# Phase differences in the first convolution, and the group 2 and 3 attention work placed between the first gates

## The chip, the cores and the metric

One core of one Trainium2 chip runs the whole kernel. The metric is the device time of one execution in microseconds; a lower time is better. The median of three runs is the time of a kernel, and one execution was recorded by the hardware profiler.

## The reference, cut to what matters

64 graphs of 128 nodes with 128 features each, all float32. Layer 0 is a gated update that reads a convolution and an attention over each graph; layer 1 is an adjacency product.

```python
h = maximum(layernorm(x), 0)
# layer 0, per graph
c  = relu(bn1(conv1(h)))            # kernel size 1
c  = relu(bn2(conv2(c)) + h)        # kernel size 17, padding 8: x_conv
s  = h @ w_se.T + b_se              # three coordinates per node
A  = exp(-dist(s, s)) * adj
nmp = A @ relu(h @ w_msg.T + b_msg)
gi, gh = [c, nmp] @ w_ih.T + b_ih, h @ w_hh.T + b_hh
r, z = sigmoid(gi_r + gh_r), sigmoid(gi_z + gh_z)
n = tanh(gi_n + r * gh_n)
x = x + (1 - z) * n + z * h
# layer 1
h = maximum(layernorm(x), 0)
x = x + adj @ (h @ weight) + bias
```

## The kernel before

**Tiles and groups.** Four graphs make a group (512 columns), so there are 16 groups. Two groups, 2t and 2t+1, are convolved together (8 graphs). The body is an opening, which brings in groups 0 to 3 and convolves groups 0 and 1, then seven steps `step(t)`, t = 1 to 7, and an ending. Step t convolves and gates groups 2t and 2t+1, brings in groups 2t+2 and 2t+3 (turn, first convolution, messages, rows, distances, neighbour sums) and finishes groups 2t-2 and 2t-1. Each product that needs accuracy is made of three TensorE passes: the operands are split in a rounded part (`_hi`, made by ScalarE) and the rest (`_lo`, made by VectorE).

**The convolution.** The nodes of a graph are stored by phase, that is by node number modulo 4, in `c1` (4 phases with 8 graphs). The 17 taps are stored by their number modulo 4: A0, A1, A2, A3 hold four taps each and T16 the last. In the steps the convolution is computed from sums of taps (M22, M12, M32, M21, M23) and differences of phases (`px`, made by GpSimd in `pre`), with fewer products. In the opening it is computed tap by tap: `direct(tap)` adds one tap to the banks pQ (even output phases) and pP (odd ones), each 512 columns wide: three passes a bank at 512 columns, or six at 256. There are 17 taps and two banks, so 34 bank products of three passes. The rounded weights live in `conv_hi`, the rests in `conv_lo`; `W_PARTS` says in which pieces they are split (`round_w` on ScalarE, `split_w` on VectorE). GpSimd makes the sums of taps in `sum_phases`.

**Order.** Every engine works off one written list in order: `opening()`, `step(t)` and `ending()` exist once for TensorE (`pe`), ScalarE (`act`), VectorE (`dve`) and GpSimd (`pool`). An instruction waits for semaphores (`wait_ge`, `have`), and everything behind it on its engine waits with it. SyncE issues the loads; those of x groups 5 to 7 wait for `gate_split`.

**Names for the steps below.** For a group g: `first(g)` (ScalarE) normalises into `hn`; `x_turn(g)` (TensorE) turns it; `hidden(g)` is `hidden_graphs` and `hidden_rows` (three ScalarE instructions); `hidden_lo(g)` (VectorE); `conv1(g)` and `conv1_out(g)`; `messages(g)` (TensorE, then ScalarE) with `place_bias(g)` and `coordinates(g)`; `pair_rows(g)` (nine small VectorE instructions), `rows_turn(g)`, `left_rows(g)`, `right_rows(g)`, `distances(g)`, `decay(g)`, `masked(g)`, `neighbour_sums(g)`, `sums_hi(g)`, `sums_lo(g)`; the gates `gates_h`, `gates_n`, `gates_c` (nine passes each), `hidden_gate`, `reset_gate`, `update_gate`, `candidate`, `blend_start(g)` and `blend_end(g)` (VectorE, three and two instructions), `o_turn(g)`, `residual(g)`. `normalise1([a, b])` (VectorE) takes the statistics of two groups, `scale1` (GpSimd) their power -0.5 and `shift1` (VectorE) the offset that `first` needs.

```python
def x_turn(g):
    have(pe, hn_set, g + 1)
    if g % 2 == 0:
        have(pe, nlo_set, g if g > 2 else 0)
        have(pe, hlo_set, 1 if g == 2 else 0)
```

## Time and profile before

| | |
|---|---|
| median of 3 runs | 346.11 us (343.37 to 346.34) |
| the profiled execution | 344.95 us, of which the span from the first to the last instruction is 342.6 us |
| TensorE passes | busy 329.8 us, 96% of the span, 2198 instructions |
| VectorE | busy 261.6 us, 76%, 735 instructions |
| ScalarE | busy 220.5 us, 64%, 431 instructions |
| GpSimd | busy 152.1 us, 44%, 131 instructions |
| mean granted TensorE clock | 0.995 of full speed |

A share is the busy time of an engine over the span. Since an engine works off its list in order, a share does not say which engine holds the others; the idle times with their releasers and the chain of waits do.

### The profile page before, as it was taken

How to read it: one execution, taken by the hardware profiler on the slowest of the kernel's cores; microseconds unless marked ns; L12 is line 12 of the kernel's file. 1: busy time of each engine (PE TensorE's matmuls, PEld its weight loads, DVE VectorE, ACT ScalarE, POOL GpSimd, SP SyncE). 2: the span in 40 equal slices, each digit the busy share in tenths (PEclk: the TensorE clock that was granted, in tenths of full speed). 3: DMA queues.
4: the chain of work that ended last, by engine and by line, in shares of the span. 5: the costliest groups of instructions: out<-in, count | busy, mean ns of one | idle time of the engine just before them, and what ended most of it. 6: DMA issues, size and time to landing. Idle time of an engine off the chain costs nothing.

```text
span 342.6 us, 6310 instructions
## 1 busy us (share of the span) xinstructions
PE 329.8 (96%) x2198; PEld 296.3 (86%) x2198; DVE 261.6 (76%) x735; ACT 220.5 (64%) x431; POOL 152.1 (44%) x131
## 2 busy tenths in 40 slices
PE   7699979999999999999999999999999999999995
PEld 5489958799988999899988999889988998899894
DVE  5576896899688995899688995899687895784474
ACT  2938835876865876676865876676866763444353
POOL 7053271024952189024952189024950189029014
PEclk9989999999999999999999999999999999999999
DMA  7900020001220022001210023001100000000003
GB/s 234 340 5 0 6 89 0 2 1 33 92 64 0 2 83 76 29 0 33 94 62 0 2 71 114 2 0 33 64 32 2 0 33 31 2 1 2 0 1 123
DMA packets 7951, 15.02 MB, mean 44 GB/s; under 512 B 1008, under 2 KB 1648, under 8 KB 7792
## 3 DMA queue, kind: packets, MB, share of 16 engines
q1 hardware_dynamic: 7776, 14.62, 12.7%
q8 instruction: 17, 0.28, 0.4%
q14 instruction: 14, 0.11, 0.1%
q10 hardware_dynamic: 144, 0.01, 0.0%
HBM read 10.43 MB, written 4.19 MB: 43 GB/s over the span
## 4 chain that ended last, share of the span: by engine, by line
PE 65%; DVE 19%; ACT 9%; issue 4%; POOL 1%; DMA 1%; POOLq 0%; DVEq 0%; ACTq 0%
PE pQ L311 4%; PE pQ L312 4%; PE pQ L313 4%; PE pNR L311 4%; PE pNR L313 4%; PE pNR L312 4%; PE pF L424 4%; PE pP L311 4%; PE pP L312 4%; PE pP L313 4%; DVE st L981 3%; ACT work L750 2%; PE pZ L484 2%; PE pI L313 2%; PE pI L311 2%
## 5 line engine op out<-in xcount | busy, mean ns | idle before, releaser
L1331 POOL TENSOR_TENSOR rs<-ve,neg_half 128x4 f32<-128x4 f32 x15 | 15.6, 1040 | 90.6 <-DVE ve L1111 90.6
L1326 POOL TENSOR_TENSOR rs<-ve,neg_half 128x8 f32<-128x8 f32 (+1 forms) x9 | 15.5, 1721 | 73.1 <-DVE ve L988 73.1
L311 PE MATMUL pP<-cx_hi,conv_hi 128*128 128x256 f32 x154 | 45.0, 292 | 0.0
L313 PE MATMUL pP<-cx_hi,conv_lo 128*128 128x256 f32 x154 | 43.5, 282 | 0.0
L312 PE MATMUL pP<-cx_lo,conv_hi 128*128 128x256 f32 x154 | 43.3, 281 | 0.0
L311 PE MATMUL pQ<-cx_hi,conv_hi 128*128 128x256 f32 x126 | 37.0, 293 | 0.0
L750 ACT ACTIVATE work<-work,nb,rs 128x128 f32<-128x128 f32 x60 | 24.8, 483 | 17.5 <-DVE nb L1115 17.0
L312 PE MATMUL pQ<-cx_lo,conv_hi 128*128 128x256 f32 x126 | 35.4, 281 | 0.0
L313 PE MATMUL pQ<-cx_hi,conv_lo 128*128 128x256 f32 x126 | 35.3, 281 | 0.0
L311 PEld LDWEIGHTS pP<-cx_hi,conv_hi 128*128 128x128 f32 x154 | 29.1, 189 | 0.3
L312 PEld LDWEIGHTS pP<-cx_lo,conv_hi 128*128 128x128 f32 x154 | 29.1, 189 | 0.3
L313 PEld LDWEIGHTS pP<-cx_hi,conv_lo 128*128 128x128 f32 x154 | 29.0, 188 | 0.0
L1069 DVE TENSOR_TENSOR cx_lo<-px,cx_hi 128x576 fp32r<-128x576 f32 x28 | 27.2, 1008 | 0.8 <-ACT cx_hi L664 0.8
L312 PEld LDWEIGHTS pQ<-cx_lo,conv_hi 128*128 128x128 f32 x126 | 23.8, 189 | 0.3
L311 PEld LDWEIGHTS pQ<-cx_hi,conv_hi 128*128 128x128 f32 x126 | 23.8, 189 | 0.0
L313 PEld LDWEIGHTS pQ<-cx_hi,conv_lo 128*128 128x128 f32 x126 | 23.7, 188 | 0.0
L770 ACT ACTIVATE work<-pNR,rz_b 128x512 f32<-128x512 f32 x16 | 11.0, 689 | 19.5 <-PE pNR L313 19.0
L683 ACT ACTIVATE hn<-x_ring,nb,rs 128x128 f32<-128x128 f32 x56 | 22.5, 485 | 0.0
L1379 POOL TENSOR_TENSOR x_ring<-work,late 128x512 f32<-128x512 f32 x16 | 20.5, 1284 | 0.3 <-DVE nb L1279 0.3
L664 ACT ACTIVATE cx_hi<-px 128x576 fp32r<-128x576 f32 x28 | 17.6, 674 | 3.5 <-POOL px L966 3.1
L399 PEld LDWEIGHTS pNR<-early,hn 128*128 128x128 f32 x128 | 16.3, 189 | 3.0 <-issue 2.1
L779 ACT ACTIVATE work<-work,vec 128x512 f32<-128x512 f32 x16 | 11.6, 724 | 11.2 <-DVE work L1083 11.2
(287 smaller groups left out, 1058.0 us busy)
## 6 DMA issues: line engine op xcount, KB each, us to landing
x_ring<-x_in SPq DMA_DIRECT2D x16, 256.0 KB, 2.8
adj_ring<-adj_in SPq DMA_DIRECT2D x16, 256.0 KB, 3.0
out<-x_ring SPq DMA_DIRECT2D x15, 256.0 KB, 2.0
work<-conv_in SPq DMA_DIRECT2D x1, 1088.0 KB, 7.6
x_ring<-gate_in SPq DMA_DIRECT2D x1, 576.0 KB, 7.7
out<-x_ring SPq DMA_DIRECT2D x2, 128.0 KB, 1.8
early<-early_in SPq DMA_DIRECT2D x1, 129.5 KB, 4.5
late<-late_in SPq DMA_DIRECT2D x1, 128.0 KB, 7.9
```

The lines of the kernel that those rows point to most:

```text
L311: pe.matmul(acc, w_hi, m_hi, start=start, stop=False)
L312: pe.matmul(acc, w_hi, m_lo, start=False, stop=False)
L313: return pe.matmul(acc, w_lo, m_hi, start=False, stop=stop)
L399: last = pe.matmul(ms[:, j, 0:MS], graph(hn[g % 2], j), w_ms, start=False, stop=True, skip_group_check=True)
L424: last = pe.matmul(lane(sums_bank(g)[:], j), graph(msg[g % 2], j), graph(att[g % 2], j), start=True, stop=True)
L664: act.activation(cx_hi[:, CX_PARTS[k][0]:CX_PARTS[k][1]], cx_source(k), ACT.Copy).then_inc(cxhi_set, 1)
L683: last = act.activation(graph(hn[g % 2], j), xs(g, j), ACT.Identity, bias=nb1[:, i:i + 1], scale=rs1[:, i:i + 1])
L750: last = act.activation(graph(h2[g % 2], j), graph(x1[g % 2], j), ACT.Relu, bias=nb2[g % 2][:, j:j + 1], scale=rs2[g % 2][:, j:j + 1])
L1069: dve.tensor_tensor(cx_lo[:, part], cx_source(k), cx_hi[:, part].bitcast(F32), ALU.subtract)\
L1326: pool.tensor_tensor(rs1[:, lane], ve1[:, lane], neg_half[:, lane], ALU.pow).then_inc(rs1_set, 1)
L1331: pool.tensor_tensor(rs2[g % 2][:], ve2[g % 2][:], neg_half[:, 0:GG], ALU.pow).then_inc(rs2_set, 1)
L1379: pool.tensor_tensor(xs(g).rearrange("p (g d) -> p g d", g=GG), x1[g % 2].rearrange("p (g d) -> p g d", g=GG), l1_bias, ALU.add).then_inc( ...
```

## The change

The first convolution (groups 0 and 1) goes over to phase differences: one sum of taps is formed from A0+A1 and A2+A3 (stored at M21, M23), `even_tap` applies the even taps to the difference of phases (8 bank products into pQ), `sum_tap` applies the summed taps to the odd phases (8, into pP), T16 is added, VectorE adds what pP holds to both `base` tiles (`with_sum`), and then `odd_tap` writes pP anew (8, with T16). So there are 26 bank products of three passes. VectorE makes the two differences (`less_odd`, `next_less_odd`) and all sums of taps (`sum_odd`, `sum_halves`), which GpSimd no longer does. Four pieces of `cx` are split instead of two, and the weights in seven parts instead of six. The row turns, distances and neighbour sums of groups 2 and 3 move from the middle of the tap products to places between the gates of groups 0 and 1 on TensorE, and the lists of ScalarE, VectorE and GpSimd are put in a new order with them. In the diff below the indentation is cut by eight; in the lists of the openings the removed lines are left out ("..."), as they stand in the listing above.

```diff
@@ -234,22 +235,36 @@
 def taps(n, first=0):
     return slice(first * D, (first + n) * D)
-W_PARTS = (taps(8, A0), taps(8, A2), taps(1, T16), taps(4, M22), taps(8, M12), taps(8, M21))
-W_SUMS = (0, 0, 0, 2, 2, 3)
+W_PARTS = (taps(4, A0), taps(4, A2), taps(1, T16), taps(8, M21), None, taps(4, M22), taps(8, M12))
+W_SUMS = (0, 0, 0, 1, 0, 3, 2)
+def w_part(w, k):
+    if k == 4:
+        return w[:, taps(16, A0)].rearrange("p (a b w) -> p b a w", a=2, b=2)[:, 1]
+    return w[:, W_PARTS[k]]
 CX_PARTS = ((X22, X22 + 1), (X12, X21 + 1), (X32, X23 + 1), (X11, X31 + 1), (X13, X33 + 1))
 CX_PRES = (0, 1, 2, 4, 5)
-FIRST_ORDER = (0, 3, 4, 1, 2)
-SLOT = (0, 2, 1, 3)
+FIRST_FILLS = (None, 3, 4, 0, 4)
 CX_FILLS = (0, 1, 2, 4, 4)
 def cx_before(t):
-    return 2 + 5 * (t - 1) if t else 0
+    return 4 + 5 * (t - 1) if t else 0
 def pre_before(t):
     return 5 * (t - 1) if t else 0
+FIRST_AT = (X11, X32, X12, X13)
+def first_source(k):
+    return (px[:, 0:2], c1[:, 2:4], c1[:, 0:2], px[:, 2:4])[k]
+def first_place(t, k):
+    return t[:, FIRST_AT[k]:FIRST_AT[k] + 2]
 def cx_source(k):
...
@@ -320,24 +335,27 @@
                                  start=j == 0, stop=j == len(weights) - 1)
         return last
-    def direct(tap, start=False, stop=False):
-        w = T16 if tap == 16 else 4 * (tap % 4) + tap // 4
+    def half_rate(bank, part, w, j, start=False, stop=False):
         w_hi, w_lo = conv_hi[:, w * D:(w + 1) * D], conv_lo[:, w * D:(w + 1) * D]
-        ends = []
-        for e, bank in enumerate((pQ, pP)):
-            at_even, at_odd = e + tap, e + 2 + tap
-            slots = [SLOT[at_even % 4], SLOT[at_odd % 4]]
-            if slots[1] == slots[0] + 1 and at_even // 4 == at_odd // 4:
-                parts = [(bank[:], slice(slots[0], slots[0] + 2), at_even // 4)]
-            else:
-                parts = [(bank[:, 0:CG * QN], slice(slots[0], slots[0] + 1), at_even // 4),
-                         (bank[:, CG * QN:], slice(slots[1], slots[1] + 1), at_odd // 4)]
-            for acc, phases, at in parts:
-                m_hi, m_lo = cx_hi[:, phases, :, at * GG:at * GG + QW], cx_lo[:, phases, :, at * GG:at * GG + QW]
-                ends.append((pe.matmul(acc, w_hi, m_hi, start=start, stop=False),
-                             pe.matmul(acc, w_hi, m_lo, start=False, stop=False),
-                             pe.matmul(acc, w_lo, m_hi, start=False, stop=stop)))
-        return ends
+        x = FIRST_AT[part]
+        if j % 2 == 0:
+            parts = [(bank[:], slice(x, x + 2), j // 2)]
+        else:
+            parts = [(bank[:, 0:CG * QN], slice(x + 1, x + 2), j // 2),
+                     (bank[:, CG * QN:], slice(x, x + 1), j // 2 + 1)]
+        for acc, phases, at in parts:
+            last = split_product(acc, w_hi, w_lo, cx_hi[:, phases, :, at * GG:at * GG + QW],
+                                 cx_lo[:, phases, :, at * GG:at * GG + QW], start, stop)
+        return last
+    def even_tap(j):
+        return half_rate(pQ, 0, (A0, A2)[j % 2] + j // 2, j, start=j == 0)
+    def sum_tap(j):
+        return half_rate(pP, 1, (M21, M23)[j % 2] + j // 2, j, start=j == 0, stop=j == 6)
+    def odd_tap(j):
+        return half_rate(pP, 3, (A1, A3)[j % 2] + j // 2, j, start=j == 0)
     def four(first, more=False):
...
@@ -377,6 +395,7 @@
             have(pe, hlo_set, 1 if g == 2 else 0)
         elif g > 1:
             have(pe, hlo_set, g)
+            have(pe, hG_set, g)
         for j in range(GG):
             last = pe.transpose(lane(turn_bank(g)[:], j), graph(hn[g % 2], j), ident[:])
         last.then_inc(hT_placed, 1)
@@ -404,6 +423,7 @@
         have(pe, pair_set, g + 1)
         if g % 2 == 0 and g > 1:
             have(pe, hlo_set, g + 2)
+            have(pe, hG_set, g + 2)
         elif g > 1:
             have(pe, c1_set, g + 1)
...
@@ -507,63 +527,73 @@
         messages(0)
         keep_clock(6)
         pe.wait_ge(w_split, 1)
+        pe.wait_ge(cxlo_set, 1)
+        even_tap(0)
+        even_tap(2)
+        even_tap(4)
+        even_tap(6)
+        messages(1)
+        pe.wait_ge(w_split, 2)
+        even_tap(1)
+        even_tap(3)
+        even_tap(5)
+        even_tap(7).then_inc(f_done[0], 1)
+        pe.wait_ge(w_split, 4)
         pe.wait_ge(cxlo_set, 2)
...
+        sum_tap(0)
         rows_turn(0)
...
+        sum_tap(2)
+        sum_tap(4)
+        rows_turn(1)
+        sum_tap(1)
+        distances(0)
+        sum_tap(3)
+        distances(1)
+        sum_tap(5)
+        sum_tap(7)
+        neighbour_sums(0)
+        sum_tap(6).then_inc(f_done[1], 1)
+        pe.wait_ge(cxlo_set, 3)
+        half_rate(pQ, 2, T16, 8, stop=True).then_inc(f_done[3], 1)
+        neighbour_sums(1)
         x_turn(2)
...
+        pe.wait_ge(w_split, 5)
+        pe.wait_ge(cxlo_set, 4)
+        pe.wait_ge(t0_set, 2)
+        odd_tap(0)
+        odd_tap(2)
+        odd_tap(4)
         conv1(2)
...
+        x_turn(3)
+        odd_tap(6)
         messages(2)
...
+        odd_tap(1)
+        odd_tap(3)
         conv1(3)
...
+        odd_tap(5)
         messages(3)
+        odd_tap(7)
+        half_rate(pP, 1, T16, 8, stop=True).then_inc(f_done[4], 1)
+        gates_h(0)
         rows_turn(2)
...
+        gates_n(0)
         distances(2)
...
+        gates_c(0)
         rows_turn(3)
...
+        gates_h(1)
+        neighbour_sums(2)
         distances(3)
...
+        gates_n(1)
         neighbour_sums(3)
...
+        gates_c(1)
+        o_turn(0)
         x_turn(4)
...
+            pe.wait_ge(w_split, 7)
...
-        elif k in (1, 2):
-            have(act, f_done[4], 1)
+        elif k:
+            act.wait_ge(f_done[FIRST_FILLS[k]], 1)
         act.activation(cx_hi[:, CX_PARTS[k][0]:CX_PARTS[k][1]], cx_source(k), ACT.Copy).then_inc(cxhi_set, 1)
-    def split_hi_phases(e):
-        act.wait_ge(c1_set, 2)
-        act.activation(cx_hi[:, 2 * e:2 * e + 2], c1[:, 2 * e:2 * e + 2], ACT.Copy).then_inc(cxhi_set, 1)
+    def split_hi_first(k):
+        if k in (0, 3):
+            act.wait_ge(diff_set, 2 if k else 1)
+        else:
+            act.wait_ge(c1_set, 2)
+        act.activation(first_place(cx_hi, k), first_source(k), ACT.Copy).then_inc(cxhi_set, 1)
...
-        have(act, hlo_set, g + 1 if g < 2 else 0)
+        have(act, hlo_set, g + 1 if g < 4 else 0)
         act.activation(hn[g % 2][:].rearrange("p (g n) -> p g n", g=GG),
                        turn_bank(g)[:].rearrange("p (n g) -> p g n", g=GG), ACT.Relu).then_inc(hG_set, 1)
...
-            have(act, cxlo_set, cx_before(g // 2 - 1) + 1 if g > 2 else g)
+            have(act, cxlo_set, (0, 3, cx_before(g // 2 - 1) + 1)[min(g // 2, 2)])
+            have(act, diff_set, g if g == 2 else 0)
...
         place_bias(0)
         hidden_graphs(0)
         conv1_out(0)
...
+        conv1_out(1)
         act.wait_ge(conv_loaded, 16)
         round_w(0)
...
+        split_hi_first(0)
+        hidden_graphs(1)
         round_w(1)
...
         messages(0)
         place_bias(1)
+        split_hi_first(1)
+        round_w(2)
+        round_w(3)
+        split_hi_first(2)
         residual_phases(0)
...
         residual_phases(1)
         act.wait_ge(gate_loaded, 16)
         act.activation(gate_hi[:], gate, ACT.Copy).then_inc(gate_rounded, 1)
         first(2)
+        messages(1)
+        place_bias(2)
         left_rows(0)
...
         left_rows(1)
         decay(0)
...
+        first(3)
+        round_w(4)
+        decay(1)
+        split_hi_first(3)
+        sums_hi(0)
+        hidden_rows(2)
+        sums_hi(1)
+        hidden_graphs(2)
         conv1_out(2)
...
         messages(2)
         place_bias(3)
+        hidden_rows(3)
+        hidden_graphs(3)
+        conv1_out(3)
+        conv_round(0, 0)
+        messages(3)
+        split_hi(1, 0)
         round_w(5)
...
+        conv_round(0, 1)
+        hidden_gate(0)
         left_rows(2)
         decay(2)
...
         reset_gate(0)
         update_gate(0)
         candidate(0)
+        left_rows(3)
+        round_w(6)
+        hidden_gate(1)
+        sums_hi(2)
+        decay(3)
         split_hi(1, 1)
         split_hi(1, 2)
...
+        first(4)
+        sums_hi(3)
+        split_hi(1, 3)
         reset_gate(1)
         place_bias(4)
         update_gate(1)
+        hidden(4)
+        first(5)
+        split_hi(1, 4)
...
-    have(eng, cxlo_set, cx_before(t) if t > 1 else 0)
+    have(eng, cxlo_set, cx_before(t))
...
-    def split_lo_phases(e):
-        have(dve, cxhi_set, e + 1)
-        dve.tensor_tensor(cx_lo[:, 2 * e:2 * e + 2], c1[:, 2 * e:2 * e + 2], cx_hi[:, 2 * e:2 * e + 2].bitcast(F32),
-                          ALU.subtract).then_inc(cxlo_set, 1)
+    def split_lo_first(k):
+        dve.wait_ge(cxhi_set, k + 1)
+        dve.tensor_tensor(first_place(cx_lo, k), first_source(k), first_place(cx_hi, k).bitcast(F32), ALU.subtract)\
+           .then_inc(cxlo_set, 1)
+    def less_odd():
+        dve.wait_ge(c1_set, 2)
+        dve.tensor_tensor(px[:, 0:2], c1[:, 0:2], c1[:, 2:4], ALU.subtract).then_inc(diff_set, 1)
+    def next_less_odd():
+        dve.tensor_tensor(px[:, 2:3], c1[:, 1:2], c1[:, 2:3], ALU.subtract)
+        dve.tensor_tensor(px[:, 3:4, :, 0:QR - GG], c1[:, 0:1, :, GG:QR], c1[:, 3:4, :, 0:QR - GG], ALU.subtract)\
+           .then_inc(diff_set, 1)
+    def sum_odd():
+        dve.wait_ge(conv_loaded, 16)
+        two_by_two = conv[:, taps(16, A0)].rearrange("p (a b w) -> p a b w", a=2, b=2)
+        dve.tensor_tensor(conv[:, taps(8, M21)].rearrange("p (a w) -> p a w", a=2), two_by_two[:, :, 0],
+                          two_by_two[:, :, 1], ALU.add).then_inc(wsum_set, 1)
+    def sum_halves():
+        dve.tensor_tensor(conv[:, taps(8, M12)], conv[:, taps(8, A0)], conv[:, taps(8, A2)], ALU.add)\
+           .then_inc(wsum_set, 1)
+        dve.wait_ge(wsum_set, 2)
+        dve.tensor_tensor(conv[:, taps(4, M22)], conv[:, taps(4, M12)], conv[:, taps(4, M32)], ALU.add)\
+           .then_inc(wsum_set, 1)
+    def with_sum(e):
+        dve.wait_ge(f_done[1], 1)
+        dve.wait_ge((sumE_set, sumO_set)[e], 1)
+        dve.scalar_tensor_tensor(base[e][:], phases(1), bn_a[:, 1:2], base[e][:], ALU.mult, ALU.add).then_inc(t0_set, 1)
     def split_lo(t, k):
-        have(dve, cxhi_set, cx_before(t) + (FIRST_ORDER.index(k) if t == 1 else k) + 1)
+        have(dve, cxhi_set, cx_before(t) + k + 1)
         part = slice(*CX_PARTS[k])
         dve.tensor_tensor(cx_lo[:, part], cx_source(k), cx_hi[:, part].bitcast(F32), ALU.subtract)\
            .then_inc(cxlo_set, 1)
     def split_w(k):
         have(dve, w_rounded, k + 1)
-        dve.tensor_tensor(conv_lo[:, W_PARTS[k]], conv[:, W_PARTS[k]], conv_hi[:, W_PARTS[k]].bitcast(F32),
-                          ALU.subtract).then_inc(w_split, 1)
+        dve.tensor_tensor(w_part(conv_lo, k), w_part(conv, k), w_part(conv_hi, k).bitcast(F32), ALU.subtract).then_inc(w_split, 1)
     def blend_start(g):
...
         dve.tensor_tensor(zh[g % 2], zh[g % 2], cand[g % 2], ALU.subtract).then_inc(oT_set, 1)
     def residual(g):
+        if g == 0:
+            dve.wait_ge(w_split, 7)
         have(dve, o_placed, g + 1)
         have(dve, h2_set, g - 1)
         have(dve, x1b_set, g - 1)
@@ -1123,6 +1190,7 @@
     def conv_out(t, e):
         have(dve, f_done[3 + e], t + 1)
         have(dve, (sumE_set, sumO_set)[e], t + 1)
+        have(dve, t0_set, 0 if t else e + 1)
         dve.scalar_tensor_tensor(phases(e), phases(e), bn_a[:, 1:2], base[e][:], ALU.mult, ALU.add).then_inc(ct_set, 1)
...
         apply1(1)
         hidden_lo(0)
         hidden_lo(1)
+        sum_odd()
+        less_odd()
         split_w(0)
...
+        split_lo_first(0)
         coordinates(0)
         split_w(1)
         normalise1([2, 3])
         split_w(2)
+        split_w(3)
+        coordinates(1)
+        split_lo_first(1)
+        shift1([2, 3])
         pair_rows(0)
...
+        dve.wait_ge(gate_rounded, 1)
+        dve.tensor_tensor(gate_lo[:], gate, gate_hi[:].bitcast(F32), ALU.subtract).then_inc(gate_split, 1)
         pair_rows(1)
         right_rows(0)
+        next_less_odd()
+        right_rows(1)
+        split_lo_first(2)
+        masked(0)
+        split_w(4)
+        masked(1)
+        split_lo_first(3)
+        sums_lo(0)
+        with_sum(0)
+        with_sum(1)
         hidden_lo(2)
...
+        sums_lo(1)
         coordinates(2)
...
+        pair_rows(2)
         hidden_lo(3)
...
+        conv_out(0, 0)
+        sum_halves()
         coordinates(3)
+        conv_lo_out(0, 0)
+        conv_out(0, 1)
+        split_lo(1, 0)
+        conv_lo_out(0, 1)
         right_rows(2)
         pair_rows(3)
...
         masked(2)
+        split_w(5)
+        blend_start(0)
         right_rows(3)
+        blend_end(0)
+        sums_lo(2)
         normalise1([4, 5])
         masked(3)
...
         shift1([4, 5])
...
+        split_w(6)
         sums_lo(3)
...
         split_lo(1, 1)
         split_lo(1, 2)
...
+        residual(0)
         hidden_lo(4)
...
+        split_lo(1, 3)
+        split_lo(1, 4)
         normalise1([6, 7])
...
@@ -1361,17 +1438,6 @@
     pool.wait_ge(bnb_set, 1)
     pool.tensor_scalar(bn_half[:], bn_b[:, 1:2], 0.5, None, ALU.mult).then_inc(vecs_set, 1)
-    def sum_phases():
-        pool.wait_ge(conv_loaded, 16)
-        pool.tensor_tensor(conv[:, taps(8, M12)], conv[:, taps(8, A0)], conv[:, taps(8, A2)], ALU.add)\
-            .then_inc(wsum_set, 1)
-        pool.wait_ge(wsum_set, 1)
-        pool.tensor_tensor(conv[:, taps(4, M22)], conv[:, taps(4, M12)], conv[:, taps(4, M32)], ALU.add)\
-            .then_inc(wsum_set, 1)
-        two = conv[:, taps(16, A0)].rearrange("p (a b w) -> p a b w", a=2, b=2)
-        pool.tensor_tensor(conv[:, taps(8, M21)].rearrange("p (a w) -> p a w", a=2), two[:, :, 0], two[:, :, 1],
-                           ALU.add).then_inc(wsum_set, 1)
     def with_bias(g):
         have(pool, x1_set, g + 1)
         if g == 0:
@@ -1397,15 +1463,13 @@
             .then_inc(sumO_set, 1)
     def opening():
-        pool.wait_ge(cxlo_set, 2)
         scale1([2, 3])
-        sum_phases()
-        pre(pool, 1, 1)
-        pre(pool, 1, 2)
         pool.wait_ge(pair_set, 4)
-        for k in range(3, 6):
+        for k in range(1, 4):
             pre(pool, 1, k)
         scale1([4, 5])
+        for k in range(4, 6):
+            pre(pool, 1, k)
```

## Rows read from the trace of the kernel before

**Rows 1.** Windows: busy us of each engine, granted clock, DMA share, GB/s
```profile
...
18.30:20.00 1.70, 1.70 (x5) 1.32 (x4) 1.67 (x13) 0.46 (x1) 0.00 (x0) 0.51 0.00 0
20.00:21.70 1.70, 1.70 (x5) 1.32 (x4) 1.53 (x14) 0.00 (x0) 1.08 (x1) 0.50 0.04 10
...
69.44:108.00 38.56, 38.41 (x266) 35.01 (x265) 31.52 (x91) 27.16 (x55) 19.11 (x14) 1.00 0.13 42
...
```

**Rows 2.** Timeline of TensorE: start us, us, line, operation, tiles, [idle before <-releaser]
```profile
...
16.87 0.47 PE L337 MATMUL pQ<-cx_hi,conv_hi 128*128 128x512 f32 x1 [2.13 <-DVE cx_lo L1063]
...
22.68 1.05 PE L399 MATMUL pNR<-early,hn 128*128 128x131 f32 x8
...
24.96 0.40 PE L337 MATMUL pQ<-cx_hi,conv_hi 128*128 128x512 f32 x1
...
26.36 0.40 PE L337 MATMUL pQ<-cx_hi,conv_hi 128*128 128x512 f32 x1
...
44.96 0.47 PE L415 MATMUL pF<-right,left 128*128 128x512 f32 x1 [0.53 <-ACT left L737]
...
50.35 0.50 PE L415 MATMUL pH<-right,left 128*128 128x512 f32 x1 [2.00 <-ACT left L737]
...
54.39 0.40 PE L311 MATMUL pNR<-h_hi,gate_hi 128*128 128x512 f32 x1
...
69.44 0.28 PE L311 MATMUL pP<-cx_hi,conv_hi 128*128 128x256 f32 x1
...
71.21 0.60 PE L381 MATMUL pF<-ident,hn 128*128 128x128 f32 x4
...
75.04 0.66 PE L474 MATMUL pI<-ident,work 128*128 128x128 f32 x4
...
```

**Rows 3.** Timeline of VectorE, same columns
```profile
...
13.92 1.22 DVE L1074 TENSOR_TENSOR conv_lo<-work,conv_hi 128x1024 fp32r<-128x1024 f32 x1 [2.42 <-ACT conv_hi L676]
15.30 1.43 DVE L1063 TENSOR_TENSOR cx_lo<-c,cx_hi 128x576 fp32r<-128x576 f32 x2 [0.16 <-ACT cx_hi L668]
...
17.96 1.64 DVE L981 BATCH_NORM_STATS2 st<-x_ring 128x6 f32<-128x128 f32 x8
...
24.98 1.07 DVE L1028 CAST svx<-sv 128x16 fp32r<-128x16 f32 x1
26.08 2.33 DVE L1030 TENSOR_TENSOR svx<-sv,svx 128x16 fp32r<-128x16 f32 x1
...
38.49 0.16 DVE L1024 TENSOR_TENSOR sq<-sv 128x12 f32<-128x12 f32 x1
...
39.72 0.68 DVE L1059 TENSOR_TENSOR n_lo<-pZ,n_hi 128x512 fp32r<-128x512 f32 x1
...
70.57 0.69 DVE L1080 SCALAR_TENSOR_TENSOR work<-work 128x512 f32<-128x512 f32 x1
...
73.50 0.69 DVE L1092 TENSOR_TENSOR work<-work 128x512 f32<-128x512 f32 x1
...
```

**Rows 4.** Timeline of ScalarE
```profile
...
12.80 1.08 ACT L676 ACTIVATE conv_hi<-work 128x1024 fp32r<-128x1024 f32 x1
...
14.59 1.26 ACT L668 ACTIVATE cx_hi<-c 128x576 fp32r<-128x576 f32 x2
...
65.44 0.59 ACT L699 ACTIVATE h_hi<-pF 128x512 fp32r<-128x512 f32 x1
...
66.39 1.65 ACT L683 ACTIVATE hn<-x_ring,nb,rs 128x128 f32<-128x128 f32 x4
...
```

**Rows 5.** Timeline of GpSimd
```profile
...
24.72 1.30 POOL L1369 TENSOR_TENSOR work<-work 128x512 f32<-128x512 f32 x1
25.97 2.41 POOL L1372 TENSOR_TENSOR work<-work 128x1024 f32<-128x1024 f32 x1
...
46.52 1.42 POOL L964 TENSOR_TENSOR ac<-c 128x576 f32<-128x576 f32 x1 [1.27 <-DVE pair L1039]
...
51.13 1.65 POOL L1326 TENSOR_TENSOR rs<-ve,neg_half 128x8 f32<-128x8 f32 x1 [0.37 <-DVE ve L988]
...
```

101 lines of the change are left out of this document (3 added, 98 removed).

## Prediction

> **What bounds the kernel now.** I read the page first: TensorE is busy for 96% of the span, the others for 44 to 76%. Then windows: in the first step it is busy for 38.41 of 38.56 us [rows 1], so the steps hold nothing that a lost microsecond could be made up from. What TensorE gains or loses before or inside step 1 stays in the total. The change touches only the stretch up to there. The timeline of TensorE gives its milestones [rows 2]: the tap products start at 16.87, the gates of group 0 at 54.39, step 1 at 69.44, x_turn(5) at 71.21, o_turn(1) at 75.04. Its losses are the idle 2.13 ahead of the first product, waits of 0.53 and 2.00 for the left rows of groups 2 and 3, and the stretch at half clock from about 18.3 to 21.7 (0.51 and 0.50 granted [rows 1]), where seven to eight passes took 0.43 instead of 0.23, a loss of 1.6. VectorE's timeline shows that group 1's blend starts at 70.57 and ends at 74.19 (73.50 + 0.69 [rows 3]), 0.85 ahead of o_turn(1): that margin is the first thing a late VectorE eats.
>
> **Prices.** All are distances from start to start. Six passes of 512 columns take 1.40 (24.96 to 26.36 [rows 2]), so a bank product of three is 0.70; six passes of 256 columns are taken the same. The eight message passes take 0.81 [rows 2] and a little behind them, 0.9; neighbour sums, which are eight passes too, the same. For VectorE: 1024 columns 1.14 to 1.22, 576 columns 0.67 to 0.75, 512 columns 0.60 to 0.69, the statistics of two groups 2.43 (17.96 to 20.39, of which 1.64 is in the row), a pair_rows 1.25 (38.49 to 39.72) [rows 3]. For ScalarE: 1024 columns 0.95 to 1.08, 576 columns 0.58, 512 columns 0.49 to 0.60, one first(g) 1.55 to 1.65 [rows 4]. GpSimd: 1.42 for a difference of phases, 1.65 for the power of eight [rows 5]. I lay the new lists of the four engines side by side, starting each instruction at the later of its engine and what it waits for.
>
> **TensorE up to the first gates.** The start moves: c1 of group 1 is ready at 13.3 since its hidden_graphs is put behind it, less_odd 0.75, rounding 0.7, the rest 0.75, and the first product starts at 15.75, 1.1 earlier. Before, 54.39 - 16.87 = 37.5 were 34 x 0.70 = 23.8 of products, 1.6 of clock, 2.5 of waits and 9.6 of other work, of which 1.7 (rows, distances, neighbour sums of groups 2 and 3) is moved behind. After: 15.75 + 26 x 0.70 (18.2) + 7.9, plus new waits. With idle time of only 1.1 ahead I count no clock loss. The waits: 0.55 for pair_rows(1) and 0.35 for right_rows(1), behind the gate_lo split and next_less_odd on VectorE; 0.5 for masked(1), which stands behind split_w(4), and that behind ScalarE's first(3) and round_w(4), done at 29.7; 1.25 before odd_tap(0), because both with_sum (0.66 each) must have read pP and stand behind masked(1), split_lo_first(3) and sums_lo(0): done at 34.15; 2.2 before conv1(3). That last one is a new wait in a queue: ScalarE does messages(2), then place_bias(3), then hidden_rows(3). TensorE ends messages(2) at 39.3, coordinates 0.1, the two ScalarE steps 1.3, hidden_rows twice 0.49, hidden_lo(3) 0.7: 42.6, and TensorE was ready at 40.5. Sum 4.85, so the gates of group 0 start at 46.5 to 46.7, 7.8 earlier than 54.39.
>
> **Between the gates.** The distances of group 2 are done only at 51.25, behind gates_n(0); before, everything of groups 2 and 3 was over by 57. Now VectorE and ScalarE carry rows, decays, masks, blend, splits and the statistics of groups 4 and 5 at the same time. Group 0's last gate is done at 53.3, the candidate at 55.3. Behind it ScalarE has left_rows(3) 0.16, round_w(6) 0.95, hidden_gate(1) 0.57, sums_hi(2) 0.59: 57.5. VectorE then does sums_lo(2) 0.6, normalise1([4, 5]) 2.43, masked(3) 0.7: 61.2. TensorE was ready for neighbour_sums(3) at 58.6: a wait of 2.7. Next, GpSimd's power of groups 4 and 5 (1.65) ends at 62.4, shift1 at 62.6, first(4) at 64.3, sums_hi(3) at 64.8, sums_lo(3) at 65.55; x_turn(4), moved behind o_turn(0), waits 0.8 for it. Step 1 starts at 66.1, now 3.3 ahead of 69.44. The weights' last split (M12, 63.8) is in time.
>
> **Step 1.** ScalarE goes on without a gap from 62.7: split 0.6, reset_gate(1) 0.63, place_bias(4) 0.65, update_gate(1) 0.63, hidden(4) 1.5, first(5) 1.65: 70.2. The change put hidden(4) and first(5) behind all of these. TensorE reaches x_turn(5) at 67.85 and waits to 70.3, 2.5 long; that is already 0.9 ahead only. VectorE meanwhile waits for hidden(4) to 68.7 and, in split_lo(1, 4), for first(5) and the split behind it to 70.8: 71.5. Then normalise1([6, 7]) 2.43, blend_start(1) and blend_end(1) 3.6: 77.6, against 74.19 before. TensorE has done conv1(4), messages(4) and the M12 product by 74.2 and waits 3.5 for o_turn(1): 77.7, 2.6 behind 75.04. hidden_lo(5) and place_bias(5) come late too, 1.0 against 0.2: 3.4 to 3.5 behind. From there the lists are those of before and every engine is late by like amounts.
>
> **What the layout leaves out.** Laid out in the same way, the kernel before (with its 1.6 of clock) comes to the gates, to step 1 and to o_turn(1) 1.1 too early each, so the like-for-like difference is +4.5. Left out as well is that VectorE and GpSimd block one another: svx's 16 elements took 2.33 and ended at 28.41, when GpSimd's addition ended (28.38), and the one before it 1.07, up to the end of the addition at 26.02 [rows 3, 5]. Moving sum_phases to VectorE takes these away (3 us of VectorE, where it had time to spare) for 1.22 + 1.22 + 0.6 of VectorE's own, where it has less. In the new order GpSimd's three differences run from 51.0 to 55.3 beside split_w(5) and blend_start(0), and two more run beside shift1 and split_w(6). Each meeting costs up to 1.42 [rows 5], four of them 5.4; what a meeting costs before as well goes off, and with all of them in both layouts the difference is +6.3. The bounds of this are 0 and 1.8, and I take a third of it, since the order in which two lists meet shifts by tenths: +5.0. The span goes from 342.6 to 347.6; with the 2.35 around it that is 350.0. The sum stands on the profiled 344.95, which is 1.2 under the median of 346.11 and inside the spread of the three runs.
>
> **The other small edits.** One more weight piece and two more cx pieces cost ScalarE 1.2 and VectorE 1.4, and sit in the queues above. Loads of x groups 5 to 7 are issued behind gate_lo, at 24 instead of 41.7; nobody waits for them, and they hide behind the products. The hG waits on turns of later groups are met earlier by hlo: nothing.
>
> **A rule of the Trainium skill.** After 2.13 idle the clock fell; after 2.00 idle at 50.35 [rows 2] it did not. The Trainium skill (TensorE: Matmul & The Clock Gate, "Part 1: The HAM clock gate") says that the engine falls to half clock once it has been idle, and gets it back by being busy. By that rule the four new waits of over 2 us are each exposed to another 1.6, and one or two of them would bring the sum to 351.6 or 353.2.
>
> **Rivals.** (1) Forecast, VectorE and ScalarE late in the first gates and in step 1, 348 to 352: 0.55. (2) More than that: a clock drop behind one of the waits (1.6, the loss of the row at half clock) or all meetings with GpSimd (1.8 on the 4.5), 352 to 356: 0.13. For it speak the long waits; against it, that a pass at half clock ahead of a wait only shortens the wait. (3) About the same: normalise1([6, 7]) and split_lo(1, 4) do not hold the blend, because first(4) and first(5) come 2 us earlier than I have them; then o_turn(1) waits 1 to 1.5 and the sum is +2 to +2.5, 347: 0.15. The layout's error of 1.1 over 50 us leaves room for that. (4) Faster: TensorE keeps its lead at step 1. Its work is 5.6 smaller (8 x 0.70), it starts 1.1 earlier, and the clock loss may go. If first(5) is there by 67.9 and group 1's blend by 74.2 - 2.5 = 71.7, the lead of 3.3, less the 1.1, stays: 342.8; if the new waits between the gates go as well, up to 5.6 + 1.1 + 1.6 = 8.3 are won: 336.7. It decides in VectorE's list: the blend would have to end six microseconds before my 77.6. For it speaks that VectorE has 12 us of waits in the opening of before; against it, that 7 us of new work take much of that and that the waits of the new order are for ScalarE and TensorE, which extra room doesn't shorten: 0.17. That the products would not shrink is excluded by the count of 26.
>
> **Numbers.** The predicted time is that of (1), 350.0. The range runs from 344.5 to 355: it leaves out (4) and the end of (2). A median of this kernel tells about 1% (3.5 us) from no change. Faster by over 1%, under 342.6: most of (4), 0.13. Slower by over 1%, over 349.6, would be half of (1) if the time were spread evenly around 350, but its mechanism leans up by the clock and GpSimd, so with (2) I give 0.55. The rest is 0.32.
>
> **What the profile after would show.** First product near 15.8 and no half-clock stretch; the first of the nine gate passes of group 0 near 46.6; a wait of 2 us before conv1(3) put down to h_lo; a wait of 2.7 before neighbour_sums(3) put down to att; step 1 near 66 to 67; waits at x_turn(5) (hn) and at o_turn(1) (work); group 1's blend ending at 77 to 79; then steps of 38.6. Wrong would make me: the blend of group 1 before 73, or an order on ScalarE in which first(4) is not held by the statistics of groups 4 and 5.

## The result, and the profile after

After: 353.51 us, the median of 5 runs (352.50 to 354.76). Before, beside it: 344.80 us (5 runs, 343.37 to 346.34). The ratio is 1.0231 with an interval of 1.0192 to 1.027, so the change made the kernel slower by about 8.7 us, where 5.0 was forecast. The profiled execution of after took 353.09 us, its span 351.3.

The page of after: span, busy time, granted clock in 40 slices.
```profile
span 351.3 us, 6261 instructions
...
PE 329.3 (94%) x2162; PEld 294.9 (84%) x2162; DVE 267.5 (76%) x746; ACT 222.2 (63%) x434; POOL 146.2 (42%) x128
...
PEclk9899999896999999999999999999999999999999
```
TensorE is now idle for 22 us of the span, and the clock row has dips in the slices of 8.8 us that begin at 9, 61 and 79.

The timeline of TensorE after: the milestones of [rows 2], and its waits between the gates and in step 1 (start, us, line, operation, tiles, idle before with its releaser).
```profile
16.58 0.48 PE L326 MATMUL pQ<-cx_hi,conv_hi 128*128 128x512 f32 x1
...
43.35 0.50 PE L326 MATMUL pH<-h_hi,early_hi 128*128 128x512 f32 x1 [1.85 <-DVE h_lo L1047]
...
47.16 0.39 PE L326 MATMUL pNR<-h_hi,gate_hi 128*128 128x512 f32 x1
...
59.07 0.47 PE L435 MATMUL pH<-right,left 128*128 128x512 f32 x1 [2.03 <-DVE right L1085]
...
64.36 1.16 PE L444 MATMUL pF<-att,msg 128*128 128x128 f32 x8 [1.48 <-DVE att L1094]
...
69.84 0.63 PE L400 MATMUL pF<-ident,hn 128*128 128x128 f32 x4 [1.76 <-DVE n_lo L1098]
70.23 0.36 PE L326 MATMUL pP<-cx_hi,conv_hi 128*128 128x256 f32 x1
...
74.47 0.66 PE L400 MATMUL pF<-ident,hn 128*128 128x128 f32 x4 [2.23 <-ACT hn L716]
...
81.81 1.13 PE L494 MATMUL pI<-ident,work 128*128 128x128 f32 x4 [3.30 <-DVE work L1157]
...
88.42 0.39 PE L435 MATMUL pF<-right,left 128*128 128x512 f32 x1
```
Against [rows 2]: the gates of group 0 start at 47.16 instead of 54.39, 7.2 earlier. Step 1 starts at 70.23 instead of 69.44: the lead is gone before step 1 begins. From the gates to there after takes 23.1 instead of 15.1. Of these 8.0, 4.9 are waits (2.03, 1.48 and 1.76, where before has one of 0.39), 1.7 is the work that was moved there, as the prediction counts it, and the rest of some 1.4 is the stretch at half clock from 60. Two more waits follow, 2.23 and 3.30, and o_turn(1) comes at 81.81 instead of 75.04, 6.8 late. distances(4) follows at 88.42. Of before, the same distances(4) and the first product of the next stage with adj_ring, which [rows 2] don't reach:
```profile
79.28 0.39 PE L415 MATMUL pF<-right,left 128*128 128x512 f32 x1
...
81.20 1.16 PE L484 MATMUL pZ<-adj_ring,work 128*128 128x128 f32 x8
```
distances(4) is 9.1 late (88.42 against 79.28): 2.4 more were lost in the seven microseconds after the last wait. The windows of after show how (busy us and count of each engine, granted clock, DMA share, GB/s).
```profile
60.00:62.00 2.00, 2.00 (x7) 1.53 (x6) 1.82 (x7) 2.00 (x5) 0.00 (x0) 0.51 0.00 0
82.00:84.00 2.00, 2.00 (x7) 1.44 (x7) 1.83 (x12) 1.80 (x4) 0.00 (x0) 0.50 0.00 0
84.00:86.00 2.00, 2.00 (x11) 2.00 (x10) 1.25 (x9) 0.77 (x2) 0.60 (x1) 0.50 0.00 0
100.00:140.00 40.00, 39.87 (x278) 36.53 (x278) 31.54 (x90) 28.61 (x58) 20.36 (x16) 1.00 0.16 51
```
From 82 to 86 TensorE ran at half clock (0.50 granted, the 1.2 GHz level); from 100 to 140 it was busy for 39.87 of 40, as full as a step in before [rows 1], so nothing could be made up later. The window at 60 is at half clock too, but it ends in the wait of 1.48 before neighbour_sums(3), which it shortens: in two other kernels with the same lists up to there the clock was full at 60, and this wait was 2.72 and 2.73.

VectorE of after, the blend of group 0 and what stands around it:
```profile
52.56 0.69 DVE L1094 TENSOR_TENSOR att<-pF,adj_ring 128x512 f32<-128x512 f32 x1 [0.93 <-issue]
53.17 1.88 DVE L1140 TENSOR_TENSOR conv_lo<-work,conv_hi 128x512 fp32r<-128x512 f32 x1
54.97 1.91 DVE L1145 SCALAR_TENSOR_TENSOR work<-work 128x512 f32<-128x512 f32 x1
56.92 0.69 DVE L1148 TENSOR_TENSOR work<-pI,work 128x512 f32<-128x512 f32 x1
...
65.43 1.38 DVE L1033 SCALAR_TENSOR_TENSOR nb<-mv,rs 128x8 f32<-128x8 f32 x1 [1.12 <-POOL rs L1403]
...
78.12 0.69 DVE L1145 SCALAR_TENSOR_TENSOR work<-work 128x512 f32<-128x512 f32 x1
...
81.06 0.69 DVE L1157 TENSOR_TENSOR work<-work 128x512 f32<-128x512 f32 x1
```
and GpSimd of after beside it:
```profile
51.71 1.44 POOL L997 TENSOR_TENSOR px<-c 128x576 f32<-128x576 f32 x1 [30.14 <-DVE pair L1078]
53.10 1.39 POOL L1000 TENSOR_TENSOR px<-c 128x560 f32<-128x560 f32 x1
54.46 1.87 POOL L1003 TENSOR_TENSOR ac<-c 128x576 f32<-128x576 f32 x1
63.76 1.64 POOL L1403 TENSOR_TENSOR rs<-ve,neg_half 128x8 f32<-128x8 f32 x1 [7.42 <-DVE ve L1027]
65.36 1.43 POOL L1005 TENSOR_TENSOR px<-ac,px 128x576 f32<-128x576 f32 x1
66.75 2.42 POOL L1007 TENSOR_TENSOR px<-ac,px 128x560 f32<-128x560 f32 x1
78.30 2.02 POOL L1403 TENSOR_TENSOR rs<-ve,neg_half 128x8 f32<-128x8 f32 x1 [9.13 <-DVE ve L1027]
```
Read the two side by side by their ends. The split of 512 columns (L1140) ends at 55.05, 0.56 behind the GpSimd row that ends at 54.49; the first step of the blend (L1145) ends at 56.88, 0.55 behind the next one's 56.33. They took 1.88 and 1.91, where the same line of the blend took 0.69 at 78.12: there VectorE came first, and it was GpSimd's power of groups 6 and 7, begun at 78.30, that took 2.02 instead of 1.64. The shift of 8 columns at 65.43 took 1.38 and ended at 66.81, GpSimd's addition at 66.79. The masked decay at 52.56, which reads one operand from PSUM (pF), took 0.69 beside GpSimd's row that ends at 53.15.

### The profile page after: what moved, and what is told of

Read it like the earlier page. It is cut to its first block, busy times and chain, and to the rows that moved or that the text cites. A ratio compares the mean times of both kernels' runs of the same rounds, so it can differ in the third digit from the quotient of the medians.

```text
span 351.3 us, 6261 instructions
## 1 busy us (share of the span) xinstructions
PE 329.3 (94%) x2162; PEld 294.9 (84%) x2162; DVE 267.5 (76%) x746; ACT 222.2 (63%) x434; POOL 146.2 (42%) x128
## 4 chain that ended last, share of the span: by engine, by line
PE 61%; DVE 17%; ACT 9%; issue 8%; POOL 2%; DMA 2%; POOLq 0%; SPq 0%; DVEq 0%; ACTq 0%
PE pQ L326 4%; PE pQ L327 4%; PE pQ L328 4%; PE pP L326 4%; PE pP L328 4%; PE pP L327 4%; PE pNR L326 3%; PE pNR L328 3%; PE pNR L327 3%; PE pF L444 3%; DVE st L1020 3%; PE pZ L504 2%; DMA early<-early_in 2%; ACT work L784 2%; PE pI L328 2%
## 5 line engine op out<-in xcount | busy, mean ns | idle before, releaser
L326 PE MATMUL pP<-cx_hi,conv_hi 128*128 128x256 f32 (+1 forms) x179 | 53.7, 300 | 1.1 <-DVE base L1130 1.1
L328 PE MATMUL pP<-cx_hi,conv_lo 128*128 128x256 f32 (+1 forms) x179 | 51.4, 287 | 0.0
L327 PE MATMUL pP<-cx_lo,conv_hi 128*128 128x256 f32 (+1 forms) x179 | 51.4, 287 | 0.0
L326 PE MATMUL pQ<-cx_hi,conv_hi 128*128 128x256 f32 (+1 forms) x139 | 41.8, 300 | 0.0
L327 PE MATMUL pQ<-cx_lo,conv_hi 128*128 128x256 f32 (+1 forms) x139 | 39.9, 287 | 0.0
L328 PE MATMUL pQ<-cx_hi,conv_lo 128*128 128x256 f32 (+1 forms) x139 | 39.8, 287 | 0.0
L326 PEld LDWEIGHTS pP<-cx_hi,conv_hi 128*128 128x128 f32 x179 | 33.9, 189 | 1.8 <-issue 1.3
L327 PEld LDWEIGHTS pP<-cx_lo,conv_hi 128*128 128x128 f32 x179 | 33.8, 189 | 0.5
L328 PEld LDWEIGHTS pP<-cx_hi,conv_lo 128*128 128x128 f32 x179 | 33.7, 188 | 0.4
L997 POOL TENSOR_TENSOR px<-c 128x576 f32<-128x576 f32 x7 | 10.0, 1432 | 30.1 <-DVE pair L1078 30.1
```

The costliest lines, as they stand in the source:

```text
L326: pe.matmul(acc, w_hi, m_hi, start=start, stop=False)
L327: pe.matmul(acc, w_hi, m_lo, start=False, stop=False)
L328: return pe.matmul(acc, w_lo, m_hi, start=False, stop=stop)
```

## The experiments

Each is one edit to the kernel after, if nothing else is said, and each ratio is to the kernel before, run beside it (344.74 to 344.81 us in these). The order is that of the questions.

**1. Which half of the change costs?** One kernel keeps the half-rate products and takes the placement back, the other keeps the products of before and takes the placement. Half-rate products are those of the changed first convolution, 26 instead of 34. The placement taken back, on TensorE (the lists of the others follow it; the statistics of groups 4 and 5 go ahead of coordinates(2), and GpSimd's first differences stand behind the power of these groups again):
```diff
 conv1(3)
+rows_turn(2)
 odd_tap(5)
 messages(3)
+distances(2)
 odd_tap(7)
+rows_turn(3)
 half_rate(pP, 1, T16, 8, stop=True)
+distances(3)
+neighbour_sums(2)
 gates_h(0)
-rows_turn(2)
+neighbour_sums(3)
 gates_n(0)
...
```
Products alone, placement taken back. 

> Half-rate products alone: row turns, distances and neighbour sums of groups 2 and 3 go back ahead of the gates, with the lists of ScalarE, VectorE and GpSimd to match. Theory: the lateness between the gates and in step 1 goes, and the 5.6 us of products are won less new waits at the odd taps (2 to 3 us): 2 to 4 us under the kernel before (341 to 343). Rival (VectorE's new work is the cost): 2 us or more over the kernel before.

Measured: 345.84, ratio 1.0045 (1.0018 to 1.0071), 1.1 us over before, so the gain of 2 to 4 us expected of the products didn't come either, and neither did the rival's loss of 2 or more.

Placement alone, products of before (the diff is to the kernel before, TensorE's list; the others follow):
```diff
-rows_turn(2)
...
-distances(2)
...
-rows_turn(3)
...
-distances(3)
-neighbour_sums(2)
...
 gates_h(0)
-neighbour_sums(3)
+rows_turn(2)
 gates_n(0)
+distances(2)
 gates_c(0)
+rows_turn(3)
 gates_h(1)
-x_turn(4)
+neighbour_sums(2)
+distances(3)
 gates_n(1)
-o_turn(0)
+neighbour_sums(3)
 gates_c(1)
+o_turn(0)
+x_turn(4)
```


> The kernel before with only the placement changed: all tap products as before, rows, distances and neighbour sums of groups 2 and 3 between the first gates as in the changed kernel, other lists to match. Theory (the placement is the cost): 4 to 8 us over the kernel before (349 to 353), with waits before neighbour_sums(3), x_turn(4), x_turn(5) and o_turn(1). Rival (the half-rate part is the cost): within 1.5 us of the kernel before.

Measured: 352.00, ratio 1.0217 (1.0182 to 1.0252), inside what was expected: the placement costs 7.3 with these lists of the other engines, with waits of 2.93 before neighbour_sums(3) (att), 1.39 before x_turn(5) (hn) and 1.81 before o_turn(1) (work) in its trace. With the products added to it (353.51) it is 1.5 more, and with the products alone 1.1 more than before. The two sum up to 8.4 for the 8.7 of the whole change. Each of the three kernels has lists of its own on the other engines, though, so these are costs of a placement or a product together with its lists.

The wait at which the products' gain is lost, in the kernel with the products alone, and its clock:
```profile
74.48 1.13 PE L494 MATMUL pI<-ident,work 128*128 128x128 f32 x4 [3.35 <-DVE work L1157]
```
```profile
74.00:76.00 2.00, 1.51 (x6) 1.41 (x7) 1.82 (x7) 1.80 (x4) 0.00 (x0) 0.50 0.00 0
76.00:78.00 2.00, 2.00 (x9) 1.54 (x8) 1.88 (x15) 1.45 (x3) 0.00 (x0) 0.50 0.00 0
```
Step 1 starts at 65.36 here, 4.1 ahead of 69.44 [rows 2]. 3.35 of it go in one wait for group 1's blend. VectorE in this kernel, from the last split of cx to the end of that blend:
```profile
67.70 0.76 DVE L1135 TENSOR_TENSOR cx_lo<-px,cx_hi 128x576 fp32r<-128x576 f32 x1 [2.03 <-ACT cx_hi L694]
68.38 1.64 DVE L1020 BATCH_NORM_STATS2 st<-x_ring 128x6 f32<-128x128 f32 x8
...
70.80 0.69 DVE L1145 SCALAR_TENSOR_TENSOR work<-work 128x512 f32<-128x512 f32 x1
...
73.74 0.69 DVE L1157 TENSOR_TENSOR work<-work 128x512 f32<-128x512 f32 x1
```
It ended the blend at 74.43, later than before's 74.19 [rows 3], because it had to wait 2.03 for ScalarE's part of the last split of cx and then did the statistics of groups 6 and 7 first. And behind the wait, the clock is at half.

**2. GpSimd beside VectorE.** The three differences of GpSimd that ran beside the split and the blend need only c of groups 2 and 3; the wait in front of them holds them back to 51.7. Without it they start at 44.4, and nothing else moves:
```diff
 scale1([2, 3])
-pool.wait_ge(pair_set, 4)
 for k in range(1, 4):
     pre(pool, 1, k)
```


> The changed kernel with GpSimd's first three phase differences freed of the wait for pair_rows(3), so that they run from about 45 to 50 instead of 51.7 to 56.3. Theory (VectorE was blocked by them for 2.4 us at split_w(5) and blend_start(0)): those two take 0.69 each, right_rows(3) and the wait before distances(3) come 1.5 to 2.4 us earlier, time 1 to 2.5 us under the changed kernel. Rival (the blocking fell in time that VectorE would have waited anyway): within 0.5 us.

Measured: 349.66, ratio 1.0136 (1.0095 to 1.0178), 3.9 less than after. VectorE and TensorE in it, the same instructions as in the fences above:
```profile
52.38 0.68 DVE L1140 TENSOR_TENSOR conv_lo<-work,conv_hi 128x512 fp32r<-128x512 f32 x1
52.98 0.69 DVE L1145 SCALAR_TENSOR_TENSOR work<-work 128x512 f32<-128x512 f32 x1
```
```profile
61.16 1.16 PE L444 MATMUL pF<-att,msg 128*128 128x128 f32 x8 [2.57 <-DVE att L1094]
...
71.27 0.66 PE L400 MATMUL pF<-ident,hn 128*128 128x128 f32 x4 [2.19 <-ACT hn L716]
...
78.61 0.74 PE L494 MATMUL pI<-ident,work 128*128 128x128 f32 x4 [3.30 <-DVE work L1157]
```
The split is down from 1.88 to 0.68, the blend's first step from 1.91 to 0.69, and the wait before distances(3) is gone. The clean measure is against a kernel that has the same lists up to there and started its products at 15.94 (the second of question 3): its x_turn(5) comes at 73.83, this one's at 71.27 from a start at 15.80. That is 2.4, and 1.20 + 1.22 of VectorE were taken out. I had expected 1 to 2.5. The profiled spans differ by 3.5 (351.3 and 347.8): 2.4 of this, and 0.8 for the later start of the profiled execution of after. The medians differ by 3.9, more than expected, and some 1.5 of it is not accounted for. Part can be the clock, whose mean was 0.970 to 0.985 in the executions of after and 0.985 to 0.990 in these; whether the other executions of after start late too, no trace tells.

**3. The statistics ahead of the blend.** Two kernels put statistics elsewhere. In the first, those of groups 4 and 5 fill VectorE's wait before coordinates(2), and their scale goes ahead of GpSimd's differences:
```diff
 sums_lo(1)
+normalise1([4, 5])
 coordinates(2)
 pair_rows(2)
+shift1([4, 5])
...
 sums_lo(2)
-normalise1([4, 5])
 masked(3)
-shift1([4, 5])
```


> The changed kernel with the statistics of groups 4 and 5 (normalise1, scale1, shift1) done in VectorE's wait of 3.7 us before coordinates(2), and GpSimd's power ahead of its differences. Theory (queues late in the first gates): the waits before neighbour_sums(3) (1.5) and before x_turn(4) (1.8) go, first(4) starts near 62.2 instead of 66.8, the waits at x_turn(5) and o_turn(1) come 4 to 6 us earlier; time 5 to 6 us under the changed kernel (347.5 to 349). Rival (VectorE's 7 us of new work for the half-rate products are the cost wherever they stand): no more than 1.5 us under it.

Measured: 350.64, ratio 1.0183 (1.0155 to 1.0211), 2.9 less than after; 5 to 6 was expected. The waits before neighbour_sums(3) and x_turn(4) are gone, x_turn(5) waits 1.40, but the wait before distances(3) is 2.51 now (2.03 in after): it is GpSimd's, not the statistics'. And in the profiled execution the clock was at half behind the wait of 1.85 before conv1(3), where after had full clock:
```profile
44.00:46.00 2.00, 2.00 (x11) 2.00 (x10) 1.14 (x2) 0.98 (x2) 0.00 (x0) 0.50 0.00 0
```
So the gates start at 48.13, where kernels with the same TensorE list and the same start have them at 46.52. These 1.6 are a part of what is missing, and they are the clock's.

In the second, those of groups 6 and 7 stand behind group 1's blend:
```diff
 split_lo(1, 4)
-normalise1([6, 7])
...
 blend_end(qq)
+if t == 1:
+    normalise1([6, 7])
```


> The changed kernel with normalise1 of groups 6 and 7 (2.4 us) behind group 1's blend in step 1 instead of ahead of it. Theory: o_turn(1) comes 2.4 us earlier (79.4) and the time falls by 2 to 2.5 us. Rival (VectorE is simply overloaded up to the middle of step 1): the 2.4 us come back at the next wait, less than 0.7 us won.

Measured: 352.17, ratio 1.0233 (1.0203 to 1.0264). The medians differ by 1.3, the ratios (1.0231 for after) not at all.
```profile
78.73 0.75 PE L494 MATMUL pI<-ident,work 128*128 128x128 f32 x4 [0.87 <-DVE work L1157]
...
81.77 0.50 PE L326 MATMUL pH<-h_hi,early_hi 128*128 128x512 f32 x1 [2.29 <-DVE h_lo L1047]
```
The wait for the blend falls from 3.30 to 0.87, and 2.29 of it come back one step later, before conv1(5): hidden_lo(5) stands behind the statistics now. The work of 2.4 us was put behind one consumer and in front of the next. Behind this wait of 2.29 the granted clock is 0.54 (82 to 84).

**4. The clock behind a long wait.** Products on the identity (the trace counts two passes for each; the results are not used) keep TensorE busy in its waits. All three waits filled, generously:
```diff
 neighbour_sums(2)
+keep_clock(12)
 distances(3)
...
+if t == 1:
+    pe.wait_ge(tz_set, 2)
+    fill_clock(14)
 x_turn(b)
...
+if t == 1:
+    fill_clock(24)
 o_turn(qq)
```


> The changed kernel with TensorE kept busy in three of its long waits by small products into banks that are free there: 12 ahead of distances(3), 14 ahead of x_turn(5), 24 ahead of o_turn(1). Nothing else moves. Theory (the stretch at half clock behind o_turn(1), 5.5 us long, is a cost of its own of about 2.3; the stretch of 60 to 64 hid in the wait for att): granted clock 1.00 from 75 on, time 2 to 2.5 us under the changed kernel. Rival (the clock falls because VectorE holds TensorE up and costs nothing of its own): within 0.5 us of the changed kernel.

Measured: 355.07, ratio 1.0283 (1.0246 to 1.0320). This is 1.6 more than after, where 2 to 2.5 less was expected. Behind the fillings the clock stayed at 1.00, but the 24 products took 5.5 us in a wait of 3.3, and the opening had half clock from 44 to 48 (0.57), so the time says nothing on the price. The trace does: from o_turn(1) to the first product with adj_ring it is 5.83 here (86.09 to 91.92) and 8.26 in after (81.81 to 90.07), 2.4 less. A single fill of 14 before o_turn(1) says more:
```diff
+if t == 1:
+    pe.wait_ge(tz_set, 2)
+    fill_clock(14)
 o_turn(qq)
```


> The changed kernel with only 14 small products (28 passes, 3.3 us) ahead of o_turn(1), the length of the wait; the runs with more of them filled 5.4 us of a wait of 3.3. Theory: half clock behind o_turn(1) goes, 2 to 2.5 us under the changed kernel (351 to 351.5). Rival (no cost of its own): 353 to 354.

Measured: 351.70, ratio 1.0203 (1.0154 to 1.0252), 1.8 less than after by the medians; the intervals of the two ratios overlap, so the trace has to carry the reading.
```profile
79.25 3.29 PE L373 MATMUL pQ<-ident 128*128 128x128 f32 x28
82.38 0.64 PE L498 MATMUL pI<-ident,work 128*128 128x128 f32 x4
...
86.34 0.39 PE L439 MATMUL pF<-right,left 128*128 128x512 f32 x1
```
The first row is the filling (28 passes, from 79.25 to about 82.5), the second o_turn(1), the third distances(4). o_turn(1) is 0.6 later than in after, and distances(4) 2.1 earlier: from one to the other it is 3.96 here, 6.61 in after and 4.24 in before. So half clock behind the wait cost 2.4 to 2.65 there. Of the 2.1, 0.65 is the start (x_turn(5) at 73.82 against 74.47). So unused work in front of a late instruction brought the next stage 1.4 forward, although it overran: the blend was done at 81.10 and o_turn(1) started at 82.38. The same in the kernel with the products alone, with 24 of them:
```diff
+if t == 1:
+    pe.wait_ge(tz_set, 2)
+    fill_clock(24)
 o_turn(qq)
```


> The kernel with half-rate products alone plus 24 small products ahead of o_turn(1), where it waits 3.35 us and then has seven microseconds at half clock. Theory: the clock stays at 1.00 and the time falls by 2 to 3 us against the same kernel without them (to 343). Rival: no change (345.8).

Measured: 346.50, ratio 1.0048 (1.0022 to 1.0073), the same as without the fillers (1.0045). Here o_turn(1) comes 1.8 later (76.29 against 74.48), and the first product of the next stage with adj_ring 0.7 earlier (82.12 against 82.82), so the half clock cost 2.5 there, but the fillers, which overran the wait by 1.8, took most of it, and 343 was expected.

**5. Mended versions.** The kernel with the products alone, its waits mended: statistics of groups 6 and 7 earlier, the last split of cx right behind the one before it, o_turn(0) behind the last gate products.
```diff
 gates_n(1)
-o_turn(0)
 gates_c(1)
+o_turn(0)
...
 split_hi(1, 3)
+split_hi(1, 4)
 hidden_gate(1)
...
 conv_lo_out(0, 1)
+normalise1([6, 7])
 sums_lo(3)
```


> The kernel with half-rate products alone and three things taken out of the way of group 1's blend: normalise1 of groups 6 and 7 goes into VectorE's wait behind conv_lo_out(0, 1), the last split of cx follows the one before it, and o_turn(0) goes behind gates_c(1). Theory (VectorE's order, not its load, ate the 5.6 us of products): group 1's blend ends near 71.5 instead of 74.4, o_turn(1) waits under 0.5, no half clock, 340.5 to 342. Rival (load): 344.5 to 346.

Measured: 342.49, ratio 0.9918 (0.9889 to 0.9947), 0.8% faster than before, if 0.5 over what was expected. The kernel after with TensorE's list as it is, and the lists of the others mended:
```diff
 left_rows(2)
+first(4)
...
 update_gate(0)
+first(5)
...
 sums_lo(1)
+normalise1([4, 5])
 coordinates(2)
 pair_rows(2)
+shift1([4, 5])
...
 sums_lo(3)
+normalise1([6, 7])
...
-pool.wait_ge(pair_set, 4)
```


> The changed kernel with its TensorE list untouched and the other lists mended: statistics of groups 4 and 5 in the wait before coordinates(2), of groups 6 and 7 behind sums_lo(3), first(4) and first(5) in waits of ScalarE between group 0's gates, GpSimd's differences freed of pair_rows(3). Theory (where each step stands in the lists of VectorE and ScalarE is the cost, and the placement on TensorE needs it): waits before neighbour_sums(3) and at o_turn(1) under 1, at x_turn(5) 1 to 2.5, time 340 to 343. Rival (work of groups 2 and 3 between the gates is too late whatever the other lists do): 346 or more.

Measured: 342.97, ratio 0.9946 (0.9914 to 0.9977), as expected. Group 1's o_turn in each:
```profile
72.54 0.75 PE L494 MATMUL pI<-ident,work 128*128 128x128 f32 x4 [0.37 <-DVE work L1157]
```
```profile
74.51 0.75 PE L494 MATMUL pI<-ident,work 128*128 128x128 f32 x4 [0.82 <-DVE work L1157]
```
Waits of 0.37 and 0.82 where after has 3.30, and from 60 to 88 both show a granted clock of 1.00. So once the other lists are mended, the placement on TensorE costs nothing that can be measured (342.97 against 342.49): some 10 us lie between the kernel after and one with the very same list on TensorE.

How far they are under before depends on the clock. The executions of before fall in three levels: a span of 341.1 to 341.3 with a mean granted clock of 0.999 or 1.000, of 342.6 to 343.1 with 0.994 or 0.995, and of 344.2 to 344.4 with 0.990. Each level is about 1.6 longer, as much as the stretch at half clock in the opening costs [rows 1]. With TensorE's list of after mended, six of ten executions had 1.000, with spans of 340.5 to 341.5; with the products alone mended, four of seven had 0.999 or 1.000, with 339.8 to 340.7. So at like clock the first gains some 0.4 over before and the second some 0.9, by the middle of these spans; the rest of their 1.8 and 2.3 goes with the clock, which fell less often in them.

As a control, before with the two general mends (left rows ahead of the splits, o_turn(0) behind the last gate products), in case they gain by themselves:

> Control: the kernel before, left_rows(3) and decay(3) of ScalarE ahead of the two splits that wait for GpSimd, and o_turn(0) behind gates_c(1) on TensorE; no half-rate products. Theory: the wait of 2.00 before distances(3) and the 0.39 at o_turn(0) go, 2 to 2.4 us under the kernel before (342.5). Then mending the order by itself is worth as much as the net gain of the half-rate products so far. Rival (the splits then come late for step 1): within 0.5 us of the kernel before.

Measured: 344.28, ratio 0.9990 (0.9956 to 1.0024), no change; the rival held. In it the wait of 2.00 before distances(3) [rows 2] is down to 0.31, but o_turn(0) starts at 66.76, as it does in before (66.75), the statistics behind its residual at 68.03, and the blend of group 1 at 70.46 against 70.57 [rows 3]:
```profile
70.46 0.69 DVE L1080 SCALAR_TENSOR_TENSOR work<-work 128x512 f32<-128x512 f32 x1
```
TensorE waits 1.16 for it there, and its granted clock is 0.57 from 76 to 80. Those two mends alone are therefore not what makes the mended versions faster. The third, statistics in VectorE's earlier waits, was not tried on before, so how much of their gain the products give and how much the order stays open.

## Why the prediction was right in direction and short in size

**Right, by its own steps.** The gates: 46.5 to 46.7 laid out, 47.16 in the trace, of which 0.7 is a half-clock stretch from 13 to 16 in that one execution (the first product at 16.58; 15.79 to 15.95 in the other traces with these products). With TensorE's list of after, the gates come at 46.37 to 46.52 in three of these traces, and at 48.13 to 48.88 in the three others, where the clock fell to half behind the wait before conv1(3). That 46.5 fits so well is in part luck, as the ledger below shows. The waits before them were 0.27, 0.40, 1.08 and 1.85 against 0.55, 0.35, 1.25 and 2.2; the one of 0.5 for masked(1) didn't come. Behind them, the chain as it was told: neighbour_sums(3) waits for att, x_turn(4) for n_lo, x_turn(5) for hn, o_turn(1) for work, at 3.30 against 3.5, because ScalarE holds first(5) behind everything:
```profile
66.84 1.65 ACT L716 ACTIVATE hn<-x_ring,nb,rs 128x128 f32<-128x128 f32 x4 [4.66 <-DVE nb L1033]
...
72.76 1.65 ACT L716 ACTIVATE hn<-x_ring,nb,rs 128x128 f32<-128x128 f32 x4
```
That placement alone gives the loss without the products, and that moving first(4), first(5) and the statistics (with GpSimd's differences) takes it away, was the forecast's mechanism (1) and is shown by three kernels. Its size was not right: 353.51 lies above the 348 to 352 of (1). Nor did all its signs come: step 1 was to start near 66 to 67 and started at 70.23, and group 1's blend was to end at 77 to 79 and ended at 81.75. One sum of its step 1 is incomplete: the ScalarE terms listed from 62.7 give 68.4, and only with first(4) and sums_hi(3), which are not in the list, about the 70.2 it goes on with.

**The step that was mis-sized is "What the layout leaves out".** The forecast bounded the meetings of GpSimd and VectorE, in which one engine's instruction holds up the other's, by 0 and 1.8 and took a third. Three of them lay on the chain to first(4): the split (1.19 over its 0.69), the blend's first step (1.22), the shift (1.23 over 0.15), 3.6 together. They also made right_rows(3) late, which gave the wait of 2.03 before distances(3) that the forecast didn't have. Laid out, first(4) was to end at 64.3; it starts at 66.84 and ends near 68.5: 4.2 late, and 3.6 is that, most of the rest the late start. From there on the layout holds again to a tenth: x_turn(5) at 74.47 for 70.3, o_turn(1) at 81.81 for 77.7, 4.2 and 4.1 late. Taking away the first two gave 2.4 back, their size; the third was not taken away by itself.

**The clock was priced at nothing, and cost about 2.4 us behind o_turn(1).** Rival (2) had it at 1.6, with a chance of 0.13 together with the meetings; both came, and the time lies in its range. What was argued against it, that half clock ahead of a wait only shortens the wait, is right for the stretch at 60 (it ends in a wait) and wrong for the one behind o_turn(1), where no wait is left: 2.4 us. Of the Trainium skill (TensorE: Matmul & The Clock Gate, "Part 1: The HAM clock gate") the prediction had drawn that each wait of over 2 us is exposed. The runs agree for the wait of 3.30 to 3.35 in four kernels (granted 0.50 behind it), and disagree among themselves for less: the wait of 2.23 before x_turn(5) in after was followed by 1.00, one of 2.20 at the same place in the kernel with 14 fillers by 0.50 (76 to 78), and in the control at the end of question 5 one of 1.16 (with another of 0.47 close behind) by 0.57. Before conv1(3) it is the same: the wait of 1.85 in after was followed by full clock, one of 1.84 in the mended kernel with TensorE's list of after by this (windows):
```profile
44.00:46.00 2.00, 2.00 (x9) 1.81 (x8) 1.93 (x3) 1.13 (x3) 0.13 (x1) 0.50 0.03 8
46.00:48.00 2.00, 2.00 (x15) 2.00 (x14) 0.31 (x2) 0.39 (x2) 2.00 (x2) 0.71 0.00 0
```
The same wait of 2.32 before conv1(3) was followed by 1.00 in the kernel with the products alone and by 0.60 (44 to 46) in its mended version. So the length of the wait alone doesn't tell.

**The ledger of the profiled execution.** The forecast was 3.4 (layout) + 1.1 (what the layout of before lacked) + 0.6 (a third of the 1.8 of the meetings) = 5.1, which it puts down as 5.0. Of the 1.1, 0.9 was there up to the gates: from 15.94 to gates at 46.5 it is 30.6, less 3.60 of waits 27.0, where 26.1 was laid out. But the waits were 1.25 smaller than their 4.85, and the two errors cancel by luck. What happened was 3.4 + 3.6 (the meetings) + 1.6 (the last stretch took 2.4 more than in before, and the layout had 0.8 of that) + 0.7 (the start) = 9.3, for the measured 9.1 at distances(4) and 8.7 in the span. The two terms that were mis-sized are the meetings and the clock.

**Rivals (3) and (4)** said that the blend would come in time. It ended at 81.75, and 12 us of spare time on VectorE in the opening didn't help, since none of it lay where the statistics waited: the mended lists show that it can be used (rival (4)'s 342.8 is what they reached), just not by this change.

What stays open: the price of the third meeting by itself, the 1.5 of the medians under question 2, what the statistics moved in before would give, and why waits of 1.85, of 2.2 and of 2.32 were once followed by half clock and once not; no run varied one wait in steps.

## What to carry to other kernels

Freed time on the busiest engine was worth nothing here until the producers of its next inputs were moved up as well: look for the input that comes last in the first stage without slack, and put its chain ahead in the lists of the other engines. Where GpSimd works beside VectorE, put its instructions beside VectorE's PSUM reads or waits, and count every other meeting on the critical chain at up to the full length of GpSimd's row (three cost 1.19 to 1.23 here, with rows of 1.39 to 1.87). TensorE's longest wait can cost again in the stretch behind it (here 3.3, then 2.4), so remove that one first. And compare kernels at like granted clock where it is known: here executions of one kernel differed by 3 us, in step with it.

## What was not expected of the hardware

VectorE and GpSimd shut one another out for whole instructions. The prediction had read this off the trace of before. Not expected was that three such meetings would fall on the critical chain at nearly full price. A step on 8 columns took 1.38 instead of 0.15 and ended within 0.02 of GpSimd's 1.43 (rows of 65.43 and 65.36); the split and the blend of group 0 took 1.88 and 1.91 instead of 0.69. It goes both ways: GpSimd's addition behind, at 66.75, took 2.42 where others of its size take 1.4, with VectorE's split of 1.21 from 66.73. A VectorE step with a PSUM operand was untouched (0.69 at 52.56, beside GpSimd's row from 51.71 to 53.15). The Trainium skill (SBUF — State Buffer, "🔬 SBUF: two separate sides") calls the shared pair of ports an exclusive lock for the whole instruction, taken by a VectorE step with two SBUF inputs against a GpSimd instruction that reads SBUF; the trace agrees in each of these rows.

Half clock behind a wait of 3.3 cost 2.4 to 2.65 us in after and 2.5 in the kernel with the products alone. Unused products in the wait kept the clock up. They brought the next stage 1.4 forward where they overran the wait by about 1.3, and 0.7 forward, with no gain in the time, where they overran it by 1.8.
